# Moving the third gate product and its gelu to the next pair of heads

## The chip, the cores and the metric

The kernel runs on one core of a Trainium2 chip. The metric is device time in microseconds (us) of one execution of the whole program; lower is better. Times carry a run-to-run spread, so the median of a few executions stands for a kernel.

## The reference

A gated delta-rule layer comes first (not touched here). Then a stack of six layers, each a windowed attention over 16 heads of 64, and a feed-forward part on tokens half of whose channels are shifted by one position:

```
for i in range(6):
    x = attn_layer(shift_tokens(x), Wqkv[i], ...) + x
    x = ffn_layer(shift_tokens(x), ln_g[i], ..., W2[i], b2[i]) + x

def ffn_layer(x, g, bln, W1, b1, W2, b2):
    xn = (x - mean) / sqrt(var + 1e-05) * g + bln
    a, gate = split(xn @ W1 + b1, 2)          # 341 columns each
    return a * gelu(gate) @ W2 + b2
```

x is 4 x 1024 x 128, all float32.

## The kernel before, in words

The stack is one long unrolled program (`local_layers`). Tokens are cut into 8 tiles of 128 positions x 4 batches (512 columns); with 6 layers that makes 48 tiles. A tile has 8 steps, one for each pair of heads. The step number is `g`; this text calls the step with `g % 8 == 4` "pair 4" and so on. Every engine runs its own loop over `g`, in a fixed order, and waits on semaphores for the others.

In a step TensorE does, in this order: the scores of pair g (mask product L1112, then 64 small products L1119); projection 0 of a later unit (`project`, L1103); the turned attention of g-1 (L1169); projection 1 (L1103); the first transpose of heads (`turn_heads`, L1133); the output product of g-1 (L1181); the transpose of the probabilities (L1140); projection 2 (L1103); the second transpose of heads (L1133); the 64 small products with the values (L1158); and last the feed-forward products that `ffn_products(g)` lists for the tile before (L1208 for gate and linear products, L1198 for the down product). A float32 product of 512 columns is issued as two passes.

Projections and feed-forward products share two PSUM banks, `a_bank(n) = p[n % 2]`, where n counts every use in program order. Use n waits in `bank_free` until use n-2 has been read: a projection by VectorE's rotation (`prod`, L1400) or ScalarE's copy (`v_tok`, L1253), a gate product by ScalarE's gelu (L1321), a linear product by VectorE (L1498: adds the bias and multiplies by the gelu in `hid`, shown as `msk`).

The feed-forward part in a tile: mean in pair 2, variance in pair 3, three gate products in pair 4, three linear ones in pair 5, down in pair 6. The 341 columns are cut into 128, 128 and 85 rows. FC is 3.

ScalarE does in a step: square of projection 0 (L1247), the copy of the turned attention into `ot` (`take_att`, L1292), the exponentials (L1296), square of projection 1 (L1247), a copy of heads (L1277 or L1279), the copy of the probabilities (L1286), in odd steps the inverse norms (L1259, L1264), the copy of projection 2 (L1253), a copy of heads, and last its feed-forward work. All transposes of TensorE go to one bank, `turn_bank`: each waits until ScalarE has copied the one before. Gelu lies in another table set than Exp and Ln: one ACT_TABLE_LOAD stands before the first gelu (L1321), and `preload_act_table_set(LN_EXP)` (L1323) loads the other set back after the last.

VectorE does in a step: maximum and difference of the scores, rotation and sum of projection 0, rotation and sum of projection 1, the division of the attention (L1446, L1450), with the feed-forward work of its step between or behind.

Of the kernel before, what the change touches and what calls it, by code (L numbers as in the profile page):

```python
# [43 lines left out]
FC = 3  # L44
# [856 lines left out]
def ffn_products(g):  # L901
    if g < 8:
        return ()
    return {2: ("mean",), 3: ("var",), 4: tuple(("gate", i) for i in range(FC)),
            5: tuple(("lin", i) for i in range(FC)), 6: ("down",)}.get(g % 8, ())


def turns(g):
# [7 lines left out]
def local_layers(nc, sbuf, names, p, banks, y, msk, ident, c, cols, key_mask, rot, weights):  # L916
# [6 lines left out]
    with ExitStack() as ctx:  # L923
# [43 lines left out]
        def vec(i, n=P):  # L967
            return w[0:n, W_VEC + i:W_VEC + i + 1]

        a_use, t_use = {}, {}  # L970
        for g in range(FIRST, LAST):
            feed, order = g + LEAD < NIT, turns(g)
            for n in range(2):
                if feed:
                    a_use["x", g, n] = len(a_use)
            if feed:
                a_use["x", g, 2] = len(a_use)
            for name in ffn_products(g):
                a_use["c", g // 8 - 1, name] = len(a_use)
            if 0 <= g - 1 < NIT:  # L980
                t_use["att", g - 1] = len(t_use)
            if order:
                t_use[order[0]] = len(t_use)
            if 0 <= g < NIT:
                t_use["p", g] = len(t_use)
            if order:
                t_use[order[1]] = len(t_use)
# [10 lines left out]
        def a_bank(n):  # L998
            return p[n % 2]
# [26 lines left out]
        def all_layers():  # L1026
            with nc.Block(no_gpsimd_drain=True) as block:
# [56 lines left out]
                def _(pe):  # L1084
# [126 lines left out]
                    for g in range(FIRST, LAST):  # L1211
                        feed, attend, behind = g + LEAD < NIT, 0 <= g < NIT, 0 <= g - 1 < NIT
                        order = turns(g)
                        if attend:
                            scores(g)
                        if feed:
                            project(g, 0)
                        if behind:
                            turn_att(g - 1)
                        if feed:  # L1220
                            project(g, 1)
                        if order:
                            turn_heads(order[0])
                        if behind:
                            output(g - 1)
                        if attend:
                            turn_probs(g)
                        if feed:
                            project(g, 2)
                        if order:  # L1230
                            turn_heads(order[1])
                        if attend:
                            values(g)
                        for name in ffn_products(g):
                            ffn(g // 8 - 1, name)

                @block.scalar
                def _(a):
# [60 lines left out]
                    def ffn(t, k):  # L1299
                        if k == 2:  # L1300
                            n = a_use["c", t, "mean"]
                            a.wait_ge(a_free[n % 2], n // 2 + 1)
                            if t:
                                n = a_use["c", t - 1, "down"]
                                a.wait_ge(a_done, n + 1)
                            a.activation(hid[:, 0, :], xc[:], ACT.Square).then_inc(sq1_ready, 1)
                        elif k == 3:
                            n = a_use["c", t, "var"]
                            a.wait_ge(a_done, n + 1)
                            a.activation(hid[:, 1, :], a_bank(n), ACT.Ln, bias=c(C_EPS))\  # L1310
                                .then_inc(a_free[n % 2], 1)
                            a.wait_ge(a_free[n % 2], n // 2 + 1)
                            a.activation(hid[:, 2, :], hid[:, 1, :], ACT.Exp, scale=-0.5).then_inc(rstd_ready, 1)
                        elif k == 4:
                            if t >= NT and t % NT == 0:
                                a.wait_ge(w1_loaded, 32 * (t // NT))
                            a.wait_ge(xn_ready, t + 1)
                            for i in range(FC):
                                n = a_use["c", t, ("gate", i)]
                                a.wait_ge(a_done, n + 1)  # L1320
                                a.activation(hid[0:FROWS[i], i, :], a_bank(n)[0:FROWS[i], :], ACT.Gelu,  # L1321
                                             bias=vec(V_GATE + i, FROWS[i])).then_inc(a_free[n % 2], 1)
                            a.preload_act_table_set(LN_EXP)  # L1323

                    a.preload_act_table_set(LN_EXP)
                    for g in range(FIRST, LAST):
                        feed, attend, behind = g + LEAD < NIT, 0 <= g < NIT, 0 <= g - 1 < NIT
                        order, U = turns(g), (g + LEAD) // 4
                        if feed:
                            square(g, 0)  # L1330
                        if behind:
                            take_att(g - 1)
                        if attend:
                            exponents(g)
                        if feed:
                            square(g, 1)
                        if order:
                            take_heads(order[0])
                        if attend:
                            take_probs(g)  # L1340
                        if feed and g % 2:
                            inverse_norms(2 * U + (g + LEAD) % 4 // 2)
                        if feed:
                            square(g, 2)
                        if order:
                            take_heads(order[1])
                        if 8 <= g:
                            ffn(g // 8 - 1, g % 8)
# [311 lines left out]
```

## Time and profile before

| | |
|---|---|
| runs | 6232.35 us median of 3 (6223.12 to 6238.5) |
| profiled execution | 6223.25 us, its span 6221.4 us |
| TensorE matmul busy | 86% of the span |
| VectorE busy | 67% |
| ScalarE busy | 44% |
| GpSimd busy | 38% |
| mean granted TensorE clock | 0.924 of full speed |
| the stack of six layers | about 2400 us to 6144 us of the span |

The stack takes about 3.7 ms, some 79 us for each of the 48 tiles. TensorE's passes overlap, so what counts is the distance from one start to the next, not the sum of durations.

### The profile page before, as it was taken

The numbers are of one execution on the slowest core, as the hardware profiler recorded it, in microseconds if no ns is written. First come the engines' busy times: TensorE is split into PE (matmuls) and PEld (weight loads), VectorE is DVE, ScalarE is ACT, GpSimd is POOL, SyncE is SP. The second block draws the span as 40 slices with busy tenths as digits, with TensorE's granted clock in tenths as the row PEclk, the third lists the DMA queues.
The fourth block names the chain that finished last, engine by engine and source line by source line (L and its number), as shares of the span: only waits on it lengthen the run. The fifth ranks groups of instructions, "written<-read, shape, count | busy, mean of one in ns | idle before, by whom it ended". The sixth has DMA issues, their size and how long they took to land. (4 is left out here: it accounts for less than half of the span.)

```text
span 6221.4 us, 170219 instructions
## 1 busy us (share of the span) xinstructions
PE 5319.4 (86%) x71376; PEld 3399.9 (55%) x71376; DVE 4155.1 (67%) x6338; ACT 2763.5 (44%) x5037; POOL 2394.6 (38%) x2148
## 2 busy tenths in 40 slices
PE   5878778686968768999999999999999999999994
PEld 4856657584857654444444555545444445445552
DVE  6565665556565657777777777777777777777772
ACT  4232231413132315555555555555555555555552
POOL 2232222222222215444444444444444444444440
PEclk8888888797878879999999999999999999999997
DMA  0000000000000002222222222222222222222221
GB/s 20 3 2 4 1 4 1 4 1 4 3 2 3 1 32 67 60 60 68 63 60 60 70 68 60 60 70 67 58 53 70 64 56 60 65 72 58 58 58 34
DMA packets 255841, 252.14 MB, mean 41 GB/s; under 512 B 29680, under 2 KB 248688, under 8 KB 254704
## 3 DMA queue, kind: packets, MB, share of 16 engines
q1 hardware_dynamic: 255088, 241.29, 15.4%
q8 instruction: 571, 9.36, 0.6%
q14 instruction: 182, 1.49, 0.1%
HBM read 29.90 MB, written 4.19 MB: 5 GB/s over the span
## 5 line engine op out<-in xcount | busy, mean ns | idle before, releaser
L1360 POOL TENSOR_TENSOR turn<-prod 128x512 f32<-128x512 f32 x768 | 983.0, 1280 | 1944.4 <-DVE prod L1400 1002.2
L1103 PE MATMUL banks<-w2s,xs 128*128 128x512 f32 x2304 | 1242.0, 622 | 97.2 <-DVE xs L1432 89.7
L1400 DVE TENSOR_TENSOR prod<-banks,tabs 128x1024 f32<-128x1024 f32 x768 | 935.6, 1218 | 114.1 <-ACT sq L1247 113.9
L1247 ACT ACTIVATE sq<-banks 128x512 f32<-128x512 f32 x768 | 458.6, 597 | 963.0 <-PE banks L1103 959.2
L1369 POOL TENSOR_TENSOR turn<-turn,rs 128x512 f32<-128x512 f32 x768 | 832.7, 1105 | 88.2 <-ACT rs L1264 84.2
L660 POOL TENSOR_TENSOR ao<-at,msk 128x512 f32<-128x512 f32 x288 | 388.0, 1358 | 1045.7 <-PE banks L412 564.2
L1133 PEld LDWEIGHTS banks<-msk,turn 128*128 128x128 f32 x3072 | 324.3, 140 | 572.4 <-issue 566.2
L1436 DVE TENSOR_REDUCE mx<-banks 128x8 f32<-128x512 f32 x384 | 265.5, 691 | 385.5 <-PE banks L1119 383.0
L1411 DVE TENSOR_REDUCE ss<-sq 128x8 f32<-128x512 f32 x768 | 518.8, 676 | 1.5
L854 DVE TENSOR_TENSOR tr<-tr,banks 128x512 f32<-128x512 f32 x240 | 165.1, 688 | 510.4 <-PE banks L436 509.1
L614 ACT ACTIVATE p<-banks 128x512 f32<-128x512 f32 x288 | 172.0, 597 | 722.4 <-PE banks L412 722.4
L1133 PE MATMUL banks<-msk,turn 128*128 128x128 f32 x3072 | 482.6, 280 | 3.4 <-ACT ot L1292 1.6
L1103 PEld LDWEIGHTS banks<-w2s,xs 128*128 128x128 f32 x2304 | 352.7, 193 | 149.8 <-DVE xs L1432 98.5
L1119 PE MATMUL banks<-kx,qt 64*32 64x64 f32 x24576 | 352.3, 224 | 89.1 <-issue 88.9
L412 PE MATMUL banks<-tr,ao 128*128 128x128 f32 x2304 | 345.9, 299 | 93.0 <-DVE tt L856 58.1
L1181 PE MATMUL banks<-ot,w2s 128*128 128x512 f32 x768 | 394.3, 595 | 3.8 <-ACT ot L1292 3.8
L1119 PEld LDWEIGHTS banks<-kx,qt 64*32 64x32 f32 x24576 | 274.2, 105 | 183.7 <-issue 183.4
L412 PEld LDWEIGHTS banks<-tr,ao 128*128 128x128 f32 x2304 | 308.2, 209 | 120.9 <-DVE tt L856 80.9
L1208 PE MATMUL banks<-xf,w2s 128*128 128x512 f32 (+1 forms) x576 | 296.9, 626 | 89.6 <-ACT msk L1321 59.7
L1286 ACT ACTIVATE pt<-banks 128x512 f32<-128x512 f32 x384 | 229.2, 597 | 311.6 <-PE banks L1140 311.6
L1158 PE MATMUL banks<-v,pt 64*32 64x66 f32 x24576 | 332.9, 225 | 2.7 <-ACT pt L1286 2.7
L1446 DVE RECIPROCAL rc<-banks 128x8 f32<-128x8 f32 x384 | 78.4, 204 | 382.5 <-PE banks L1158 382.4
(202 smaller groups left out, 9828.7 us busy)
## 6 DMA issues: line engine op xcount, KB each, us to landing
v<-v_tok SPq DMA_DIRECT2D x1152, 132.0 KB
v<-v_tok SPq DMA_DIRECT2D x384, 66.0 KB
v<-v SPq DMA_DIRECT2D x188, 132.0 KB, 2.5
w2s<-in_weights SPq DMA_DIRECT2D x10, 768.0 KB, 4.7
tabs<-in_rot SPq DMA_DIRECT2D x40, 128.0 KB, 2.7
w2s<-in_weights SPq DMA_DIRECT2D x1, 2713.5 KB, 11.0
w2s<-in_weights SPq DMA_DIRECT2D x10, 256.0 KB, 3.0
xin<-in_x SPq DMA_DIRECT2D x8, 256.0 KB, 2.9
```

Source lines behind the costliest of these rows:

```text
L412: last = pe.matmul(p[3 * x][:, b * P:(b + 1) * P], ao[:, 2 * x + i % 2, b, :], tr[:, x, b, :], start=True, stop=True)
L660: g.tensor_tensor(ao[:, 2 * x + i % 2, :, :], at[:, x, :, :], over_batches(msk[:, M_OFF + LEVELS + i, :]), ALU.mult)\
L1103: pe.matmul(a_bank(use), xs[:, t % 2, b * P:(b + 1) * P], w[:, at:at + 512], start=True, stop=True).then_inc(a_done, 1)
L1119: last = pe.matmul(sc[n * WIN:(n + 1) * WIN, h, b * 2 * WIN:(b + 1) * 2 * WIN], qt[r, j, b * P + n * WIN:b * P + (n + 1) * WIN], kx[r, j, ...
L1133: last = pe.transpose(turn_bank[:, i * P:(i + 1) * P], src[:, i * P:(i + 1) * P], ident)
L1158: last = pe.matmul(pv[n * WIN:(n + 1) * WIN, h, b, :], pt[r, g % 2, b * P + n * WIN:b * P + (n + 1) * WIN], v2[r, h2, b, n, i * DV1:(i + 1 ...
L1181: pe.matmul(out_bank, w[:, W_O + j * P:W_O + (j + 1) * P], ot[:, g % 3, :], start=(j == 0), stop=(j == NP2 - 1)).then_inc(o_done, 1)
L1247: a.activation(sq[:, r % 2, :], a_bank(use), ACT.Square).then_inc(sq_done, 1)
L1360: gp.tensor_tensor(turn[:, r % ROTS, :, :].rearrange(halves, s=2), prod[:, r % 2, 0, :, :].rearrange(halves, s=2), prod[:, r % 2, 1, :, :] ...
L1369: gp.tensor_tensor(turn[:, r % ROTS, :, :], turn[:, r % ROTS, :, :], along(rs[:, q % 2, b, :], DH), ALU.mult).then_inc(rot_done, 1)
L1400: v.tensor_tensor(prod[:, r % 2, :, :, :], a_bank(use).rearrange("p (h d) -> p h d", h=HU).unsqueeze(1) .to_broadcast([P, 2, HU, DH]), tab ...
L1411: v.tensor_reduce(ss[:, q % 2, b, :], sq[:, r % 2, :].rearrange("p (h d) -> p h d", h=HU), AX.X, ALU.add).then_inc(red_done, 1)
```

## The change

The third gate product and its gelu move from pair 4 to pair 5 of each tile, in front of the three linear products.

```
 def ffn_products(g):
     if g < 8:
         return ()
-    return {2: ("mean",), 3: ("var",), 4: tuple(("gate", i) for i in range(FC)),
-            5: tuple(("lin", i) for i in range(FC)), 6: ("down",)}.get(g % 8, ())
+    return {2: ("mean",), 3: ("var",), 4: (("gate", 0), ("gate", 1)),
+            5: (("gate", 2),) + tuple(("lin", i) for i in range(FC)), 6: ("down",)}.get(g % 8, ())
...
-                        elif k == 4:
+                        elif k in (4, 5):
                             if t >= NT and t % NT == 0:
                                 a.wait_ge(w1_loaded, 32 * (t // NT))
                             a.wait_ge(xn_ready, t + 1)
-                            for i in range(FC):
+                            for i in ((0, 1), (2,))[k - 4]:
                                 n = a_use["c", t, ("gate", i)]
                                 a.wait_ge(a_done, n + 1)
                                 a.activation(hid[0:FROWS[i], i, :], a_bank(n)[0:FROWS[i], :], ACT.Gelu,
                                              bias=vec(V_GATE + i, FROWS[i])).then_inc(a_free[n % 2], 1)
                             a.preload_act_table_set(LN_EXP)
```

The last line is inside the branch, so it now runs after the gelus of pair 4 and again after the gelu of pair 5. The bank of every use follows from the count, so the projections of pair 5 change banks.

## Rows read from the trace of the kernel before

**Rows 1.** Waits, TensorE, 2463 to 6090 us: us in total, times, longest us.

```profile
PE banks L1119 <- issue: 83.6, 92, 2.4
PE banks L1208 <- ACT msk L1321: 58.0, 46, 1.3
PE banks L1208 <- DVE prod L1400: 27.1, 46, 0.8
```

**Rows 2.** Timeline, TensorE, pairs 4 to 6 of one tile: start us, us, line.

```profile
4028.87 0.38 PE L1112 MATMUL banks<-kmask,idb 128*128 128x256 bf16 x2
...
4037.26 1.98 PE L1208 MATMUL banks<-xf,w2s 128*128 128x512 f32 x4 [0.57 <-DVE prod L1400]
4040.50 1.09 PE L1208 MATMUL banks<-xf,w2s 128*85 128x512 f32 x2 [1.26 <-ACT msk L1321]
4041.42 0.38 PE L1112 MATMUL banks<-kmask,idb 128*128 128x256 bf16 x2
...
4042.52 1.12 PE L1103 MATMUL banks<-w2s,xs 128*128 128x512 f32 x2
...
4044.91 0.63 PE L1133 MATMUL banks<-msk,turn 128*128 128x128 f32 x4
...
4049.16 3.06 PE L1208 MATMUL banks<-xf,w2s 128*128 128x512 f32 x6
4052.06 0.38 PE L1112 MATMUL banks<-kmask,idb 128*128 128x256 bf16 x2
...
4059.80 2.85 PE L1198 MATMUL banks<-msk,w2s 128*128 128x512 f32 x6
4062.49 0.38 PE L1112 MATMUL banks<-kmask,idb 128*128 128x256 bf16 x2
```

**Rows 3.** Timeline, TensorE: openings of pairs 5 and 6, first and last of 46 tiles.

```profile
2466.76 0.38 PE L1112 MATMUL banks<-kmask,idb 128*128 128x256 bf16 x2
2477.40 0.38 PE L1112 MATMUL banks<-kmask,idb 128*128 128x256 bf16 x2
...
6022.09 0.38 PE L1112 MATMUL banks<-kmask,idb 128*128 128x256 bf16 x2
6032.72 0.38 PE L1112 MATMUL banks<-kmask,idb 128*128 128x256 bf16 x2
```

**Rows 4.** Timeline, ScalarE, the same stretch.

```profile
4038.46 1.28 ACT L1321 ACT_TABLE_LOAD   x1 [1.94 <-PE banks L1208]
4039.76 1.26 ACT L1321 ACTIVATE msk<-banks,w2s 128x512 f32<-128x512 f32 x2
4041.62 0.68 ACT L1321 ACTIVATE msk<-banks,w2s 85x512 f32<-85x512 f32 x1 [0.60 <-PE banks L1208]
4042.33 1.28 ACT L1323 ACT_TABLE_LOAD   x1
4043.68 0.60 ACT L1247 ACTIVATE sq<-banks 128x512 f32<-128x512 f32 x1
4044.18 0.59 ACT L1292 ACTIVATE ot<-banks 128x512 f32<-128x512 f32 x1
...
4048.95 0.59 ACT L1277 ACTIVATE kx<-banks 128x512 f32<-128x512 f32 x1
```

**Rows 5.** Timeline, VectorE, the same stretch.

```profile
4046.05 1.22 DVE L1400 TENSOR_TENSOR prod<-banks,tabs 128x1024 f32<-128x1024 f32 x1
...
4050.33 1.61 DVE L1498 SCALAR_TENSOR_TENSOR msk<-banks,w2s,msk 128x512 f32<-128x512 f32 x2
```

**Rows 6.** Timeline, ScalarE, the last tile.

```profile
6136.83 0.68 ACT L1321 ACTIVATE msk<-banks,w2s 85x512 f32<-85x512 f32 x1 [1.52 <-PE banks L1208]
```

**Rows 7.** Windows: PE, PEld, DVE, ACT, POOL busy (instructions), granted clock, DMA share, GB/s.

```profile
4039.00:4040.00 1.00, 0.24 (x1) 0.00 (x0) 0.00 (x0) 0.99 (x2) 0.00 (x0) 1.00 0.03 10
```

**Rows 8.** Timeline, TensorE, pair 1 of another tile.

```profile
5043.50 0.80 PE L1119 MATMUL banks<-kx,qt 64*32 64x64 f32 x57 [1.86 <-issue]
5044.23 1.78 PE L1103 MATMUL banks<-w2s,xs 128*128 128x512 f32 x2
```

**Rows 9.** Windows, the stretch behind it, columns as in rows 7.

```profile
5044.00:5048.00 4.00, 4.00 (x31) 2.03 (x25) 2.71 (x4) 1.70 (x3) 0.02 (x1) 0.57 0.01 4
```

More of the change, by code:

```diff
@@ L903, in ffn_products @@
         return ()
-    return {2: ("mean",), 3: ("var",), 4: tuple(("gate", i) for i in range(FC)),
-            5: tuple(("lin", i) for i in range(FC)), 6: ("down",)}.get(g % 8, ())
+    return {2: ("mean",), 3: ("var",), 4: (("gate", 0), ("gate", 1)),
+            5: (("gate", 2),) + tuple(("lin", i) for i in range(FC)), 6: ("down",)}.get(g % 8, ())
 def turns(g):
@@ L1313, in ffn @@
                             a.activation(hid[:, 2, :], hid[:, 1, :], ACT.Exp, scale=-0.5).then_inc(rstd_ready, 1)
-                        elif k == 4:
+                        elif k in (4, 5):
                             if t >= NT and t % NT == 0:
@@ L1317, in ffn @@
                             a.wait_ge(xn_ready, t + 1)
-                            for i in range(FC):
+                            for i in ((0, 1), (2,))[k - 4]:
                                 n = a_use["c", t, ("gate", i)]
```

## The prediction

> **What bounds the kernel now.** I read the waits of TensorE over the stack first. TensorE is busy in nearly all of it, and three of the largest waits are [rows 1]: the small score products waiting for "issue" (nothing that the profile shows; I read it as late instructions), and two waits of the gate products. Of these two, the wait on the gelu comes once in each of 46 tiles, 58.0 us in all, 1.26 each. That is the one that the change touches. The second look is at the timeline of pairs 4 to 6 of one tile, engine by engine. The reader should see in [rows 2] that TensorE runs without a gap from the third gate product to the end of pair 6, so a start moved in there moves all that follows. I compared the distances between the mask products (L1112), which open each step, for the 46 tiles that have all eight pairs (first and last in [rows 3]): pair 5 takes 10.64 us and pair 6 10.42 us in nearly all, to 0.01. So one tile can stand for all; what varies (pairs 0 to 4) lies before the place of the change.
>
> **Why the third gate product waits.** The first gate product starts at 4037.26 [rows 2]. ScalarE, which had been idle for 1.94 us, begins its table load at 4038.46, when this product is done, and not earlier; the load takes 1.28, the first gelu starts at 4039.76 [rows 4], and, as one gelu lasts 0.68, it frees the bank at 4040.44. The third product, in the same bank, starts at 4040.50: 3.24 us after the first. In these 3.24 us TensorE has two products to run, four passes of 0.43, or 1.72 (the pass distance is from the down product: six passes and the start of the next mask product in 2.69 us [rows 2]). The wait, from start to start, is 3.24 - 1.72 = 1.52 us.
>
> **The change, part by part.** I follow one tile and compare the opening of pair 6, 4052.06 before.
>
> *Pair 4 to projection 0 of pair 5.* Everything up to the second gate product is unchanged. The scores of pair 5 now follow at about 4039.1 and take 1.10 (mask product to projection, 4041.42 to 4042.52), so projection 0 could start at 4040.2. But it is now the use that comes two after gate 0, so it waits for gelu 0 as the third product did, until 4040.50. Before it started at 4042.52: -2.02 us. The scores now fill most of the wait; what is left of it is 0.3.
>
> *Pair 5, first half.* ScalarE ends the second gelu at 4039.76 + 1.26 = 4041.02 and then loads the other table set back, to about 4042.33. Its next work is the square of projection 0, at about 4042.40 (it followed the load by 0.07 before). That projection was ready for it at 4040.50 + 1.16 = 4041.66 (1.16 is the distance before, 4042.52 to 4043.68). So ScalarE is 0.74 late in pair 5. What queues behind is `ot`, whose copy frees the only bank of the transposes: it ended 1.09 after the start of the square [rows 4], so now at 4043.49, and the transpose of heads came 0.14 behind it [rows 2]: 4043.62. Without the wait it would start 2.39 after projection 0, at 4042.89. The new wait costs +0.73 us. Behind it nothing else gets later: from the heads on TensorE is 0.73 late and ScalarE 0.74, so each meets the other at the distance of before, and VectorE's rotations follow the squares in the same way. From the heads to the end of pair 5's values I keep the distance of 4.25 (4044.91 to 4049.16): the feed-forward products start at 4047.87, that is 1.29 earlier than before.
>
> *Pair 5, feed-forward products.* The order is now gate 2, linear 0, 1, 2. Counted through, gate 2 takes the bank of projection 1 (rotation done in time: it ended at 4047.27 before, and moves forward with the rest [rows 5]) and linear 1 the bank of gate 2. So linear 1 waits for gelu 2, in front of which stands a table load that begins when gate 2 is done: ScalarE ends its copy of heads 0.38 after the start of these products [rows 4], so it is idle and the case is that of gate 0 again, 3.24 us. Between are again two products, 1.72. The wait of 1.52 is back, only in another place. Then linear 1 and 2, each 0.86, and the opening of pair 6 at 0.06 more. Sum: 3.24 + 0.86 + 0.92 = 5.02 us, where the three linear products took 4052.06 - 4049.16 = 2.90 (some 0.2 of it a wait for VectorE's first linear result, which ended its first two at 4051.94 [rows 5]; it is now covered). +2.12 us. The load back after gelu 2 ends about 4.6 after gate 2's start, before projection 0 of pair 6 is done, so it costs nothing; the same cover hides VectorE's work on linear 1 and 2, whose distance to the next scores stays as it was.
>
> *Sum for a tile:* -2.02 + 0.73 + 2.12 = +0.83 us. No DMA is added or moved. SyncE waits only on bank counts that move with the projections, and GpSimd, busy 38% of the span, is waited for nowhere among the large waits.
>
> *Tiles 46 and 47* have no projections. Tile 46 runs through the same two waits, with ScalarE's lateness met by the output product in place of the heads; I take +0.9. In the last tile nothing lies between gate 1 and gate 2: the third gelu started at once with its product's end (6136.83 [rows 6]) and now has its own load in front, +1.3.
>
> *Total:* 46 x 0.83 + 0.9 + 1.3 = +40.4 us. The profiled execution took 6223.25 us (span 6221.4), so 6263.6. It lies 9 us under the median of the runs; on the median it would be 6272.7. I predict between, 6268 us, +0.6%.
>
> **The table load and the Trainium skill.** In the trace the load lasts 1.28 us, the gelu follows it by 0.02, and the load back follows the last gelu by 0.03 [rows 4]. The Trainium skill (ScalarE: Activation LUTs, What ACT_TABLE_LOAD costs) gives 1283 ns for the load, and adds about 1380 ns of drain for each switch. By that, an estimate, two more switches would cost ScalarE 2.8 us more per tile. The trace shows the load and no such drain.
>
> **What the traces leave open.** Instruction supply. Score products wait for issue 92 times [rows 1], after steps with no or one feed-forward product: by the same distances over 46 tiles, pair 4, which follows one product, is on average 0.38 us over its least, pair 1, which follows none, 1.18; pairs 5 to 7, which follow three products, 0.01. Pair 5 would now follow two. Lower end: nothing, since the DMA engines are nearly done with pair 4's traffic when these scores would start, a busy share of 0.03 [rows 7]. Upper end: as pair 4, +0.38, or 17 us over the stack. I take nothing, nearest to the rows of the traffic. The Trainium skill (Runtime: NRT & Kernel Launch, Instruction fetch mechanics) says that the fetch is mostly hidden; by that this term is zero, though [rows 1] shows that it is not always so.
>
> **The rivals.**
> *A, the second load starts early (no change).* If ScalarE's load for gelu 2 ran as soon as ScalarE is free, 0.38 after gate 2's start, it would be over at 1.66, the gelu at 2.37, and linear 1 would start 0.81 earlier: +0.02 per tile, total +3, so 6226 to 6235. For it: ScalarE is idle then. Against: it was as idle in pair 4 and the load did not start until the product was done [rows 4].
> *B, linear 1 finds its bank free (faster).* If the wait in pair 5 vanished, as the move may suggest, -1.52 + 0.83 = -0.69 per tile, -32 us, 6191 to 6200. It decides for faster once the wait there is under 0.69. Against: the count of banks, and the load that stands between product and gelu.
> *C, ScalarE's lateness is hidden (about no change).* Then +0.10 per tile, +7 in all, 6230 to 6239. For it: the heads' transpose comes 0.13 after projection 1 too, so both limits are near each other. Against: 0.74 is late against at most 0.05 of slack.
> *D, instruction supply (slower still).* +1.21 per tile, +58, 6281 to 6290.
> *E, the clock falls (much slower).* In a pair 1, after an issue wait of 1.86, projections of 1.12 [rows 2] last 1.78 [rows 8], and the granted clock is 0.57 over 4 us [rows 9], that is mostly the lower of its two levels, 1.2 GHz. If the two waits in pair 5 did this in each tile, about +1.7 more, 6342 and over. Against: waits of 1.26 have not done it in any of 46 tiles, pair 5 being always 10.64.
>
> **How the numbers follow.** Chances: my forecast 0.68, D 0.14, E 0.03, A 0.05, C 0.07, B 0.03. A measurement can tell about 0.3% here, 19 us or 0.4 per tile. Forecast, D and E are slower: 0.85; A and C within: 0.11 with a little of each beyond, B faster: 0.04. The range goes from half of ScalarE's lateness hidden (6263.6 - 17 = 6247, less a little for the spread of runs: 6242) to D on the median (6290, rounded to 6292).
>
> **What the changed profile would show.** The gate wait in pair 4 gone; projection 0 of pair 5 waiting some 0.3 for gelu 0; the first transpose of heads in pair 5 waiting for `ot` some 0.7; in pair 5 a wait of linear 1 on the gelu, 1.26 by the view's reckoning; twice as many table loads as now; from the opening of pair 4 to that of pair 6 24.0 us, where it is 23.2 in the tile shown (4028.87 to 4052.06 [rows 2]). The prediction is wrong if the load for gelu 2 begins before gate 2 is done, if the heads do not wait for `ot`, or if pairs far from the change alter their lengths.

## The result and the profile after

The changed kernel takes 6272.22 us (median of 6 runs, 6257.72 to 6279.25), the kernel before 6227.74 us (6 runs, 6217.35 to 6238.5): a ratio of 1.0069, 95% interval 1.0052 to 1.0085. It is slower by about 0.7%, or 44 us between the medians. The profiled execution has a span of 6269.7 us, 48.3 more than before.

The waits of TensorE over the stack (2463 to 6135 us) in the changed kernel, with us in total, times and longest:

```profile
PE banks L1119 <- issue: 87.8, 92, 2.3
PE banks L1103 <- DVE xs L1432: 58.2, 40, 1.8
PE banks L1208 <- ACT msk L1321: 57.8, 46, 1.3
PE banks L1133 <- ACT ot L1292: 31.2, 48, 0.8
PE banks L1208 <- DVE prod L1400: 27.1, 46, 0.8
...
PE banks L1103 <- ACT msk L1321: 11.6, 45, 0.5
```

The wait of the gate and linear products on the gelu is as large as in [rows 1]: 57.8 us in 46 waits, after 58.0 in 46. It was not removed, only moved: it now stands before linear 1 in pair 5. Two lines are new among the large ones: the transpose of heads waits for `ot`, 31.2 us (1.6 in the kernel before), and a projection waits for a gelu, 11.6. The second line, projections that wait for VectorE to write `xs`, is 58.2 us in the kernel before as well; [rows 1] does not show it, and the change does not touch it.

One tile of the changed kernel on TensorE, in the timeline (start us, us, line), to be laid beside [rows 2]:

```profile
4061.33 1.98 PE L1208 MATMUL banks<-xf,w2s 128*128 128x512 f32 x4 [0.55 <-DVE prod L1400]
4063.15 0.38 PE L1112 MATMUL banks<-kmask,idb 128*128 128x256 bf16 x2
...
4064.57 1.12 PE L1103 MATMUL banks<-w2s,xs 128*128 128x512 f32 x2 [0.25 <-ACT msk L1321]
...
4067.64 0.63 PE L1133 MATMUL banks<-msk,turn 128*128 128x128 f32 x4 [0.64 <-ACT ot L1292]
...
4071.89 1.95 PE L1208 MATMUL banks<-xf,w2s 128*85 128x512 f32 x4
4075.09 1.98 PE L1208 MATMUL banks<-xf,w2s 128*128 128x512 f32 x4 [1.25 <-ACT msk L1321]
4076.91 0.38 PE L1112 MATMUL banks<-kmask,idb 128*128 128x256 bf16 x2
```

Both gate products of pair 4 run through, the scores follow at 4063.15, and projection 0 starts at 4064.57, 3.24 us after gate 0: the distance at which the third gate product stood in [rows 2]. Gate 2 opens pair 5's feed-forward work at 4071.89, linear 0 is merged into the same row, and linear 1 waits.

ScalarE in the same tile:

```profile
4062.54 1.28 ACT L1321 ACT_TABLE_LOAD   x1 [2.02 <-PE banks L1208]
4063.83 1.26 ACT L1321 ACTIVATE msk<-banks,w2s 128x512 f32<-128x512 f32 x2
4065.11 1.28 ACT L1323 ACT_TABLE_LOAD   x1
4066.41 0.60 ACT L1247 ACTIVATE sq<-banks 128x512 f32<-128x512 f32 x1
4066.90 0.59 ACT L1292 ACTIVATE ot<-banks 128x512 f32<-128x512 f32 x1
...
4073.06 1.28 ACT L1321 ACT_TABLE_LOAD   x1 [0.80 <-PE banks L1208]
4074.35 0.68 ACT L1321 ACTIVATE msk<-banks,w2s 85x512 f32<-85x512 f32 x1
4075.05 1.28 ACT L1323 ACT_TABLE_LOAD   x1
```

The load back fills the time in which the square of projection 0 should start (4066.41, 1.84 after the projection, where it was 1.16). `ot` ends at 4067.49 and the transpose follows 0.15 behind it. For gelu 2, ScalarE sits idle for 0.80 us until gate 2 is done, and only then loads the tables.

From the openings of the steps, as means over the same 46 tiles (worked out from the timelines; the least in brackets):

| | pair 4 | pair 5 | 4 and 5 | pairs 0 to 3 | tile |
|---|---|---|---|---|---|
| before | 12.92 (12.55) | 10.64 (10.63) | 23.56 | 36.83 | 79.00 |
| after | 10.60 (10.21) | 13.77 (13.75) | 24.37 | 36.98 | 79.95 |

Pairs 6 and 7 are unchanged (10.43 and 8.17). The place of the change costs 0.80 us per tile, or 37 us.

### The profile page after: what moved, and what is told of

It is laid out like the page before. It is cut to its first block and busy times, and to the rows that moved or that the text cites. A ratio compares the mean times of both kernels' runs of the same rounds, so it can differ in the third digit from the quotient of the medians.

```text
span 6269.7 us, 170363 instructions
## 1 busy us (share of the span) xinstructions
PE 5316.9 (85%) x71376; PEld 3405.5 (54%) x71376; DVE 4156.5 (66%) x6338; ACT 2886.9 (46%) x5133; POOL 2395.1 (38%) x2148
## 5 line engine op out<-in xcount | busy, mean ns | idle before, releaser
L1247 ACT ACTIVATE sq<-banks 128x512 f32<-128x512 f32 x768 | 458.6, 597 | 877.1 <-PE banks L1103 876.3
L1133 PEld LDWEIGHTS banks<-msk,turn 128*128 128x128 f32 x3072 | 324.7, 140 | 604.2 <-issue 599.3
L1133 PE MATMUL banks<-msk,turn 128*128 128x128 f32 x3072 | 482.6, 280 | 33.2 <-ACT ot L1292 31.2
L412 PE MATMUL banks<-tr,ao 128*128 128x128 f32 x2304 | 345.8, 299 | 93.6 <-DVE tt L856 58.2
L1208 PE MATMUL banks<-xf,w2s 128*128 128x512 f32 (+1 forms) x576 | 287.5, 622 | 90.4 <-ACT msk L1321 60.5
```

The costliest lines, as they stand in the source:

```text
L412: last = pe.matmul(p[3 * x][:, b * P:(b + 1) * P], ao[:, 2 * x + i % 2, b, :], tr[:, x, b, :], start=True, stop=True)
L1133: last = pe.transpose(turn_bank[:, i * P:(i + 1) * P], src[:, i * P:(i + 1) * P], ident)
L1247: a.activation(sq[:, r % 2, :], a_bank(use), ACT.Square).then_inc(sq_done, 1)
```

## The experiments

All ratios are to the kernel before, with runs on the same chip. Times per pair or tile are means over the 46 tiles of the profiled execution. The added lines shift the line numbers: in the rows below L1209 is the L1208 of the kernel before, L1134 its L1133, L1248 its L1247, and L1323 or L1324 its L1321.

**Load the gelu tables early in pair 5** (on the changed kernel). `preload_act_table_set` stands right behind ScalarE's copy of heads, ahead of its wait for gate 2.

```
+GELU = "gelu_and_others"
...
                         elif k in (4, 5):
+                            if k == 5:
+                                a.preload_act_table_set(GELU)
                             if t >= NT and t % NT == 0:
```

> The changed kernel, with the gelu tables loaded in pair 5 as soon as ScalarE has done its copy of heads, ahead of its wait for gate 2. My theory (linear 1 waits for gate 2's product, then the load, then the gelu): the load is over before the product's gelu could start or 0.5 us behind it, so linear 1 starts 0.81 us earlier; against the changed kernel -0.8 us per tile, -37 us; against the kernel before about +6 us (ratio 1.001). Rival 1 (the number of table loads costs, not their place): no change against the changed kernel, ratio 1.007. Rival 2 (the bank of linear 1 is freed by something else than gelu 2): no change either, and the wait of L1208 in pair 5 stays 1.26.

Measured: 6235.0 us, ratio 1.0016 (1.0007 to 1.0025). Pair 5 fell from 13.77 to 12.99 us, -0.78, where 0.81 was expected; the other pairs hardly moved. ScalarE and TensorE in one tile:

```profile
4057.34 0.59 ACT L1278 ACTIVATE kx<-banks 128x512 f32<-128x512 f32 x1
4057.95 1.28 ACT L1317 ACT_TABLE_LOAD   x1
4059.24 0.68 ACT L1324 ACTIVATE msk<-banks,w2s 85x512 f32<-85x512 f32 x1
```

```profile
4057.56 1.95 PE L1209 MATMUL banks<-xf,w2s 128*85 128x512 f32 x4
4059.98 1.98 PE L1209 MATMUL banks<-xf,w2s 128*128 128x512 f32 x4 [0.47 <-ACT msk L1324]
```

The load starts 0.39 us after the start of gate 2 and no longer after its end, and linear 1 follows gate 2 by 2.42 us where it was 3.20. The number of loads is the same, so rival 1 falls; the wait followed gelu 2, so rival 2 falls.

**Load the gelu tables early in pair 4** (on the changed kernel).

```
                         elif k in (4, 5):
+                            if k == 4:
+                                a.preload_act_table_set(GELU)
```

> The changed kernel, with the gelu tables loaded ahead of the wait in pair 4 only. My theory: gelu 0 and 1 and the load back end about 1 us earlier, so projection 0 of pair 5 no longer waits (0.3) and ScalarE is on time for the square and the transpose of heads (0.73): -1.03 us per tile, -47 us against the changed kernel, ratio to the kernel before about 0.999; pair 5 keeps its gate wait of 1.26. Rival (the late transpose of heads is not ScalarE's doing): only 0.3 per tile, -14 us, ratio 1.005, and the waits of L1133 on ot stay.

Measured: 6221.23 us, ratio 0.9994 (0.9984 to 1.0005). Pair 5 fell by 1.00 us to 12.77. The waits of TensorE in this kernel:

```profile
PE banks L1209 <- ACT msk L1324: 59.0, 47, 1.3
...
PE banks L1134 <- ACT ot L1293: 1.6, 2, 0.8
```

The transposes wait for `ot` twice, as in the kernel before, the projections no longer wait for a gelu, and the gate wait of pair 5 stays. So both new waits of pair 5's first half came from gelus and load back ending late. The edit moves both together; their parts (from start to start 0.32 us before projection 0 and 0.68 before the transpose, 1.00 together) are read from the timeline, not separated by a run.

**Third gate product without its gelu and loads** (on the changed kernel). The kernel leaves out the third gelu, so it does not compute the layer: ScalarE only adds the bias.

```
-  ... a_bank(n)[0:FROWS[i], :], ACT.Gelu,
+  ... a_bank(n)[0:FROWS[i], :], (ACT.Identity if i == 2 else ACT.Gelu),
...
-                            a.preload_act_table_set(LN_EXP)
+                            if k == 4:
+                                a.preload_act_table_set(LN_EXP)
```

> The changed kernel with the gelu of the third gate product left out: ScalarE copies it with the bias added, from the table set that is in place, so pair 5 has no table load at all. My theory: the bank of linear 1 is free 1.28 us earlier and 0.2 of the wait is left: -1.3 us per tile, -60 us against the changed kernel, ratio to before 0.997. Rival (it is the order of the products and the banks that costs, the load does not matter): -0.1 per tile at most, ratio 1.006.

Measured: 6196.61 us, ratio 0.995 (0.9937 to 0.9964), 76 us under the changed kernel, where 60 and 0.997 were expected: more than the interval allows. Pair 5 is at 12.49 us, -1.28: the length of one load. That term is as expected. The rest is not in pair 5: in the profiled execution pairs 0 to 3 are 0.28 us shorter together (pair 1 8.57 us after 9.03, pair 2 11.05 after 10.78), 13 us over the 46 tiles. Score products waited for issue 82 times here, 92 in the changed kernel, 74.3 us in all after 87.8.

```profile
PE banks L1119 <- issue: 74.3, 82, 2.2
```

Why these waits were shorter in this kernel was not tried, so this part of the difference stays unexplained.

**Early load in the kernel before.** The three gate products stay in pair 4.

```
                         elif k == 4:
+                            a.preload_act_table_set(GELU)
```

> The kernel before, with the gelu tables loaded ahead of the wait for gate 0. ScalarE is idle for 1.94 us there, and the load takes 1.28. My theory: gelu 0 starts when its product is done, 1.30 us earlier, and the third gate product follows 3.24 - 1.30 = 1.94 after the first: -1.3 us per tile, -60 us, ratio 0.990. Rival (a load does not go ahead of the wait, or its work collides with something else): no change, ratio 1.000.

Measured: 6171.49 us, ratio 0.9912 (0.9896 to 0.9928). Pair 4 fell from 12.92 to 11.65, -1.27. ScalarE in one tile:

```profile
4014.20 0.60 ACT L1278 ACTIVATE kx<-banks 128x512 f32<-128x512 f32 x1
4014.81 1.28 ACT L1316 ACT_TABLE_LOAD   x1
4016.82 1.49 ACT L1323 ACTIVATE msk<-banks,w2s 128x512 f32<-128x512 f32 x2 [0.72 <-PE banks L1209]
4018.68 0.68 ACT L1323 ACTIVATE msk<-banks,w2s 85x512 f32<-85x512 f32 x1 [0.38 <-PE banks L1209]
```

The load now ends 0.7 us before gate 0 is done, and the gate wait, 58.0 us in 46 waits before, is a single one of 0.3 us (2463 to 6090 us).

**Early loads in both places of the changed kernel.** Both of the first two edits.

> The changed kernel with both gelu loads ahead of their waits (pair 4 and pair 5). If the terms add, 0.8 us in pair 5 and 1.0 at its start: -1.8 per tile against the changed kernel, so -1.0 against the kernel before, -46 us, ratio 0.993. That stays behind the kernel before with the one early load (0.991), because the gate wait of pair 5 keeps 0.7 us where that of pair 4 keeps 0.2. Rival (splitting the gate products pays once the loads are hidden): ratio under 0.991.

Measured: 6186.51 us, ratio 0.9929 (0.9913 to 0.9945). Pair 5 is at 11.98 us, 1.79 under the changed kernel: the terms add. What is left of the gate wait:

```profile
PE banks L1209 <- ACT msk L1323: 23.2, 47, 1.6
```

With pairs 4 and 5 at 22.60 together it stands 0.30 us per tile behind the kernel before with one early load (22.29). The intervals of the two ratios (0.9929 and 0.9912) overlap, so this rests on the profiles. By them, splitting the gate products does not pay with early loads either.

**Two idle loads in the kernel before.** No product is moved.

```
                             a.preload_act_table_set(LN_EXP)
+                        elif k == 5:
+                            a.preload_act_table_set(GELU)
+                            a.preload_act_table_set(LN_EXP)
```

> The kernel before with two more table loads on ScalarE at the end of pair 5, and no product moved: as many loads as the changed kernel, where ScalarE is idle for 4.8 us. My theory: no change, ratio 1.000, pair 5 and 6 at 10.64 and 10.42 us. Rival (the added loads cost wherever they stand, by a drain or by their own traffic): up to 2.6 us per tile, ratio up to 1.019.

Measured: 6230.72 us, ratio 1.0001 (0.9987 to 1.0015); pairs 5 and 6 at 10.64 and 10.43 us.

```profile
4061.73 1.28 ACT L1326 ACT_TABLE_LOAD   x1
4063.02 1.28 ACT L1327 ACT_TABLE_LOAD   x1
4066.50 0.60 ACT L1248 ACTIVATE sq<-banks 128x512 f32<-128x512 f32 x1 [2.20 <-PE banks L1104]
```

The same number of loads as in the changed kernel costs nothing where ScalarE has 2.20 us left behind them. Two loads also follow each other by 1.29 us, start to start, so nothing of any length lies between them.

**Early load, and a later sum on VectorE, in the kernel before.** The experiments pointed away from the split, so this takes the other gate wait of [rows 1].

```
                             rotate(g, 0)
-                            sums(g, 0)
+                            if g < 8 or g % 8 != 4:
+                                sums(g, 0)
...
                             rotate(g, 1)
+                            if g >= 8 and g % 8 == 4:
+                                sums(g, 0)
```

> The kernel before with the early load (ratio 0.991), and in pair 4 VectorE sums the first squares after the second rotation, no longer before it. Gate 0 waits 0.57 us there for that rotation, which would end 0.6 us earlier: -0.5 to -0.6 us per tile more, -26 us, ratio 0.987. Rival (the late sum holds up ScalarE's inverse norms or squares): the gain is given back in pair 5.

Measured: 6139.89 us, ratio 0.9856 (0.9837 to 0.9876), the fastest of the kernels here. Pair 4 is at 11.01 us, another 0.64 down, and pair 5 stays at 10.64, so nothing is given back there. The gate products of pair 4 run without a wait:

```profile
4006.01 3.05 PE L1209 MATMUL banks<-xf,w2s 128*128 128x512 f32 x6
```

## Why the prediction was right, point by point

**Forecast and direction.** 6268 us was forecast, 6272 measured; for the ratio, 1.006 and 1.0069 (1.0052 to 1.0085). That the two lie only 4 us apart is in part luck. The forecast was set between two bases, and the terms give 40.4 us, while the profiled executions differ by 48.3: 37 from pairs 4 and 5 of the 46 tiles (38 forecast), 2.5 from tile 46 and 2.0 from the last tile (0.9 and 1.3 forecast), and some 7 from pairs 0 to 3, for which the forecast has no term.

**Projection 0 takes the third gate product's place, -2.02.** Right: 3.24 us after gate 0 in both kernels. What was left of its wait, from start to start, was 0.32 for the 0.3 forecast (1.42 from the mask product to the projection, where it was 1.10).

**ScalarE late, +0.73.** Right, slightly smaller. The transpose of heads starts 3.07 us after projection 0, where it was 2.39: +0.68. The square followed the load by 0.02 and not by 0.07. The early load in pair 4 takes this wait away and gives 1.00 us per tile, so rival C (the lateness is hidden) falls.

**The wait comes back in pair 5, +2.12.** Right. Gate 2 to linear 1 is 3.20 us (3.24 forecast), gate 2 to the opening of pair 6 5.02 (5.02 forecast). That it was the table load behind the product is shown twice: by loading early (-0.78) and by leaving the load out (-1.28). Rival A's price was right as well (0.81 us per tile for an early load; the first experiment gave 0.78), but in both kernels the load that the activation itself brings along started only when the product was done; to start early it had to be written ahead of the wait. Rival B (no wait) did not occur.

**Sum per tile.** +0.83 forecast, +0.80 in pairs 4 and 5. Pairs 0 to 3, far from the change, were 0.15 longer, 6 to 7 us in all; the prediction had named that as a sign of being wrong. The two idle loads moved the same pairs by 0.23 with the time unchanged within the interval, so I can't tell this part from chance. Rival D, late instructions in pair 5, did not occur: pair 5 has a mean of 13.77 with a least of 13.75. (Pair 1 of the kernel before is on average 1.20 us over its least, not 1.18; nothing rests on it.)

**Tile 46, +0.9.** Mis-sized: pairs 4 and 5 took 20.89 us after 18.44 (9.65 and 8.79), +2.45. Up to the output product all went as in the other tiles: pair 4 is 2.34 shorter, and the output product, which waits for `ot`, comes 3.91 after the opening of pair 5 where it was 2.85, so -1.28 for the two (-1.29 by the forecast's terms). The missing 1.6 us lie behind that wait:

```profile
6139.53 1.12 PE L1181 MATMUL banks<-ot,w2s 128*128 128x512 f32 x2 [2.15 <-ACT ot L1292]
...
6143.25 3.71 PE L1208 MATMUL banks<-xf,w2s 128*85 128x512 f32 x4
```

Four passes took 3.71 us instead of 1.95, and the windows view shows the granted clock at 0.50 just then (columns as in rows 7):

```profile
6135.60:6139.50 3.90, 1.77 (x71) 1.21 (x69) 1.38 (x2) 3.86 (x6) 0.00 (x0) 1.00 0.00 0
6139.50:6142.00 2.50, 1.91 (x6) 0.98 (x6) 0.00 (x0) 1.02 (x2) 0.00 (x0) 0.72 0.00 0
6142.00:6146.00 4.00, 3.88 (x68) 1.98 (x68) 0.90 (x2) 0.73 (x2) 0.00 (x0) 0.50 0.02 6
```

That is rival E, the fall of the clock, in this one tile, and the forecast gave it no place in the term of tile 46. The runs bear the cause out. In tile 46 of three kernels the output product of pair 5 waits 2.15 us for `ot`: the changed one, the one with the early load in pair 5 only, and the one without the third gelu. Over pair 5 their mean granted clock is 0.75, 0.86 and 0.75. In the other six kernels that wait is 1.08 or 1.09, and the clock is 1.00. With the early load in pair 4 of the changed kernel, pair 5 of tile 46 takes 10.92 us and not 13.58, which is 2.66 less, where the other tiles gained 1.00. Its window:

```profile
6088.35:6099.27 10.92, 7.88 (x150) 4.02 (x149) 3.69 (x6) 7.02 (x9) 0.00 (x0) 1.00 0.01 2
```

In the 46 tiles with projections the clock granted over pair 5 of the changed kernel is 1.00 in each, so rival E did not occur there.

**The last tile, +1.3.** The end of the span moved 2.0 us further than the opening of the last step (48.3 and 46.3). From the first gate product to the down product the last tile takes 10.00 us where it took 8.91, +1.1 for the 1.3 forecast. Another 0.7 stands before it: from the output product to the mean product 3.86 us after 3.15, at a granted clock of 0.50 after 0.62. The clock fell earlier there; why is not shown.

## What to carry to other kernels

A wait on a buffer goes with the count of buffers, not with the place of the work: before moving a consumer, count which use meets which buffer in the new order. Here the same 3.2 us of product, table load and gelu held back another product some 10 us later. When a wait is mostly a table load, move the load: one line ahead of the semaphore wait gave 0.9%, where moving the product lost 0.7%.

## What was not expected of the hardware

Two pieces. The clock of TensorE fell to its lower level (granted 0.50, 1.2 GHz) after a wait of 2.15 us, in a stretch where TensorE was busy for 1.77 of 3.90 us; this came in the same tile of all three kernels with that wait, and in none of the six in which it was 1.09 or less. In pair 5 of each of the 46 tiles with projections the clock stayed at 1.00; in the tile shown its waits are 0.25, 0.64 and 1.25. So 1.06 us more of waiting in one tile cost some 1.6 us beyond its own length. And the score products' waits for issue changed from kernel to kernel (82 to 95 waits, 74.3 to 91.7 us in all): pair 1 was between 8.57 and 9.03 us on average, though no edit touched it. What sets these waits is not shown. Differences of 0.1 or 0.2 us per tile in those pairs are not to be explained by an edit elsewhere.
